# Rotation tables gathered and result rows scattered by GpSimd's indirect transfers

## The reference

```python
x = x + L0_gnn(layernorm(x), adj)      # tanh filter, two 128x128 products, adj product
x = x + L0_ffn(layernorm(x))           # 8 experts 128 -> 256 -> 128, top 2 of 8 by a gate
x = x + L1_gnn(layernorm(x), adj)      # normalised (adj + I) @ x @ w, elu
x = x + L1_ffn(layernorm(x))           # causal attention, then 8 experts 128 -> 341 -> 128, top 2
# in the attention, for 4 query heads and 2 key heads of 32 dimensions:
q = q * cos + rotate_half(q) * sin
k = k * cos + rotate_half(k) * sin
```

## Time and profile before

| | |
|---|---|
| runs | 735.93, 737.3, 740.03 us; median 737.3 us |
| the profiled execution | 740.08 us, its span from the first to the last instruction 738.0 us |
| TensorE busy | 662.6 us (90%) |
| VectorE busy | 551.4 us (75%) |
| ScalarE busy | 319.7 us (43%) |
| GpSimd busy | 135.3 us (18%) |

### The profile page before, as it was taken

One profiled execution on the slowest core, in us unless ns is written; L12 is line 12 of the kernel. 1 busy time (PEld: TensorE's weight loads), 2 busy tenths in 40 slices (PEclk: granted clock), 3 DMA queues, 4 the chain that ended last, 5 costly groups with the idle time before them and its releaser, 6 DMA issues. The chain is left out here.

```text
span 738.0 us, 13217 instructions
## 1 busy us (share of the span) xinstructions
PE 662.6 (90%) x4749; PEld 339.5 (46%) x4749; DVE 551.4 (75%) x1231; ACT 319.7 (43%) x472; POOL 135.3 (18%) x178
## 2 busy tenths in 40 slices
PE   3999889999958998787899999979778999999997
PEld 2433324777744454332322322423244666666665
DVE  7898485899993366778666766682679888888886
ACT  0554305799930111021322433546445556555554
POOL 2000040243630222002060000010012142324200
PEclk9999989999997999969899999999899899999999
DMA  8950000001014011001120000000000010000001
GB/s 324 418 237 1 9 21 15 16 16 29 15 28 98 0 32 33 1 0 33 27 64 29 1 1 0 2 0 2 0 1 9 22 31 30 1 28 28 0 0 57
DMA packets 18173, 30.65 MB, mean 42 GB/s; under 512 B 5024, under 2 KB 14800, under 8 KB 15824
## 3 DMA queue, kind: packets, MB, share of 16 engines
q1 hardware_dynamic: 16672, 29.84, 12.0%
q10 hardware_dynamic: 1456, 0.22, 0.2%
HBM read 26.63 MB, written 1.05 MB: 38 GB/s over the span
## 5 line engine op out<-in xcount | busy, mean ns | idle before, releaser
L1252 PE MATMUL ps<-xT,A 128*128 128x512 f16 (+1 forms) x576 | 133.1, 386 | 7.1 <-DVEq L1764 4.3
L1648 DVE TENSOR_REDUCE A<-ps 128x1 f32<-128x512 f32 (+3 forms) x160 | 92.5, 608 | 42.3 <-PE ps L1125 41.7
L801 ACT ACTIVATE A<-ps 128x1024 f32<-128x1024 f32 (+3 forms) x80 | 68.7, 895 | 81.6 <-PE ps L1192 81.6
L1252 PEld LDWEIGHTS ps<-xT,A 128*128 128x128 f16 (+1 forms) x576 | 59.9, 107 | 67.5 <-DVEq L1764 4.8
L1774 DVE SCALAR_TENSOR_TENSOR A<-ps,A 128x512 f32<-128x512 f32 (+1 forms) x96 | 65.6, 683 | 31.8 <-ACT A L831 26.5
L831 ACT ACTIVATE A<-ps 128x512 f32<-128x512 f32 (+1 forms) x96 | 57.1, 595 | 54.6 <-PE ps L1252 54.5
L1267 PE MATMUL ps<-A 128*128 128x128 f16 (+1 forms) x1152 | 71.8, 222 | 4.1 <-DVE R L1730 2.3
L839 ACT ACTIVATE A<-A 128x512 f16<-128x512 f32 (+1 forms) x96 | 59.8, 623 | 33.6 <-DVE A L1774 33.6
L1267 PEld LDWEIGHTS ps<-A 128*128 128x128 f16 (+1 forms) x1152 | 68.6, 99 | 11.7 <-issue 2.6
L1781 DVE TENSOR_TENSOR A<-A 128x512 f16<-128x512 f32 (+1 forms) x96 | 72.0, 750 | 0.1
L566 POOL TENSOR_TENSOR A<-A,factor 128x682 f32<-128x682 f32 (+3 forms) x32 | 38.5, 1216 | 146.7 <-PE ps L1267 90.4
(11 more groups left out here) (202 smaller groups left out, 814.4 us busy)
## 6 DMA issues: line engine op xcount, KB each, us to landing
A<-in_adj_t SPq DMA_DIRECT2D x16, 1024.0 KB, 22.9
A<-in_f_w SPq DMA_DIRECT2D x16, 170.5 KB
A<-A SPq DMA_DIRECT2D x72, 32.0 KB, 1.8
R<-in_f_w SPq DMA_DIRECT2D x16, 128.0 KB, 2.1
x<-in_x_in SPq DMA_DIRECT2D x4, 256.0 KB, 4.6
R<-in_cos_t SPq DMA_DIRECT2D x4, 256.0 KB, 4.5
R<-in_sin_t SPq DMA_DIRECT2D x4, 256.0 KB, 7.9
A<-in_f_w SPq DMA_DIRECT2D x8, 128.0 KB
```

Of the source, the lines that this page charges most:

```text
L801: act.activation(Pb[:, n % 2, 2 * pair:2 * pair + 2, t0:CW], ps[:, 2 * pair:2 * pair + 2, t0:CW], ACT.Exp, scale=1.0 / (SQ * SQ * float(HD ...
L1252: last = pe.matmul(ps[0:r, 3 * m + k, :], w[:, s, m, k0:k0 + r], a[:, CW * g:CW * g + CW], start=(n == 0), stop=(n == 2))
L1648: dve.reduce_max(pm[:, h, t % TPC, b:b + 1], ps[:, bank, 0:width], AX_X).then_inc(s_rmf, 1)
```

## The change

The eight table copies by SyncE become two indirect gathers by GpSimd: for each of the 128 partitions p it reads row p mod 32 of the table. The row numbers are made by an iota on GpSimd and an AND on VectorE (`head_dim`). GpSimd waits for `s_add0` ahead of them, as SyncE did, and they raise a new semaphore, `s_tab`, for which VectorE waits beside `s_attw`. The four stores by SyncE become sixteen indirect scatters by GpSimd, one for each tile of 128 rows of 512 bytes, with the row numbers in `row_at`.

```diff
@@ -116,6 +116,8 @@
+        row_at = sb("row_at", [P, NT], I32)
+        head_dim = sb("head_dim", [P, 1], I32)
@@ -496,9 +500,6 @@
             sp.wait_ge(s_add0, E0 * NC + 2)
-            for dst, src in ((cos_sb, cos_t), (sin_sb, sin_t)):
-                for h in range(NH):
-                    sp.dma_start(dst[HD * h:HD * h + HD, :], src).then_inc(s_attw, 16)
             for dst, src in ((wq32, wq), (wk32, wk), (wv32, wv), (wo32, wo), (wr32, w_router)):
                 sp.dma_start(dst, src).then_inc(s_attw, 16)
@@ -526,10 +527,6 @@
-            for g in range(NC):
-                sp.wait_ge(s_add1, (E1 - 1) * NC + g + 1 + 2)
-                sp.dma_start(out[:, TPC * g:TPC * g + TPC, :], x[:, TPC * g:TPC * g + TPC, :]).then_inc(s_out, 16)
-            sp.wait_ge(s_out, 16 * NC)
@@ -545,6 +542,10 @@
+            pool.iota(row_at[:, :], pattern=[[1, NT]], base=0, channel_multiplier=NT).then_inc(s_const, 1)
+            pool.iota(head_dim[:, :], pattern=[[0, 1]], base=0, channel_multiplier=1).then_inc(s_const, 1)
+            pool.wait_ge(s_const, 4)
@@ -609,6 +610,13 @@
+            pool.wait_ge(s_add0, E0 * NC + 2)
+            pool.wait_ge(s_hd, 1)
+            for dst, src in ((cos_sb, cos_t), (sin_sb, sin_t)):
+                pool.indirect_dma_start(out=dst, out_offset=None, in_=src,
+                                        in_offset=bass.IndirectOffsetOnAxis(ap=head_dim[:, 0:1], axis=0),
+                                        bounds_check=HD - 1).then_inc(s_tab, 16)
@@ -653,6 +661,13 @@
             chain.loop_ends(E1 // 2 - 1, 6)
+            rows_out = out.rearrange("p t d -> (p t) d")
+            for g in range(NC):
+                pool.wait_ge(s_add1, (E1 - 1) * NC + g + 1 + 2)
+                for t in range(TPC * g, TPC * g + TPC):
+                    pool.indirect_dma_start(out=rows_out, out_offset=bass.IndirectOffsetOnAxis(ap=row_at[:, t:t + 1], axis=0),
+                                            in_=x[:, t, :], in_offset=None, bounds_check=T - 1).then_inc(s_out, 16)
+            pool.wait_ge(s_out, 16 * NT)
@@ -1409,6 +1424,8 @@
+            dve.wait_ge(s_const, 4)
+            dve.tensor_scalar(head_dim[:, :], head_dim[:, :], HD - 1, None, ALU.bitwise_and).then_inc(s_hd, 1)
@@ -1514,7 +1531,8 @@
-            dve.wait_ge(s_attw, 16 * (2 * NH + 5))
+            dve.wait_ge(s_tab, 32)
+            dve.wait_ge(s_attw, 16 * 5)
```

More of the change, by code:

```diff
@@ L238, in program @@
         s_cpool = sem("pool_steps")
+        s_hd = sem("head_dimension_ready")
+        s_tab = sem("rotation_tables_loaded")
         s_dve = sem("vector_steps")
```

## The result

The changed kernel takes 749.7 us (median of four runs, 749.1 to 757.8), the kernel before 737.6 us beside it: a ratio of 1.0183 with a 95% interval of 1.0141 to 1.0226. The loss is 12.1 us; 6.3 us were forecast. A ratio is taken over the undisturbed runs and a median over all of them, so the one need not be the quotient of the others. The profiled execution after has a span of 748.1 us, 738.0 before.

The account below looks back on a forecast made before the run. TensorE, busy 90% of the span, was taken as the bound, its last expert block's matmuls ending the chain. Stores +6.2 us, with the AND +6.3, tables 0: 737.3 + 6.3 = 743.6 us, range 739.8 to 757.0.

Parts of the forecast that it names:

- the small additions: Two iotas on GpSimd at the start, costing nothing, and one AND on VectorE at 105 us, 0.1 us on the path.
- The tables: Two gathers on GpSimd from 221.4 us, hidden in idle time, 0 us; VectorE may go on as late as 240.1.
- The rival with late tables: Second gather lands after 240.1 and TensorE waits in the second graph stage; 2 us at 8 us per gather; chance 0.05.
- The stores: Sixteen GpSimd scatters at the kernel's end, 4.4 us per chunk with a backlog, last issue at 741.64: +6.2 us.
- N: Time one scatter holds GpSimd, put at 1.1 us; between 1.06 and 1.38 the stores cost 12N - 7.0 us.
- The last L1797 "still at about 735": Sign in the profile after: VectorE's last add still at about 735 us; well after would mean port or tables.
- The rival with the shared port: VectorE and GpSimd hold each other up in the tail: +8.0 us if VectorE loses, +10.0 if GpSimd waits; chance 0.15.
- scatters of differing length while VectorE works: Sign in the tail that the forecast is wrong and the port is at work; sixteen transfers of equal length were forecast.
- the other form of the port rival: In the tail GpSimd waits for VectorE, 0.7 us for each scatter issued before 735: end at 748.0, +10.0 us.
- the cheap case: Rival at the stores: a scatter holds GpSimd no longer than SyncE's store issue, 0.34 us: +1.0 us; chance 0.17.
- the case that was thought most likely: The forecast itself, at the stores: one scatter takes 0.8 to 1.5 us, +3.7 to +11.5 us; chance 0.45.
- a slow issue: Rival at the stores: one scatter takes 2 to 3.35 us, all 16 in one line: +19.5 to +41 us; chance 0.18.

Follow-up runs that it names:

- the four wide scatters: Changed kernel with tables copied by SyncE and the stores as four GpSimd scatters of 2 KB rows instead of sixteen of 512 B: 740.5 us beside 737.9 (ratio 1.0043).
- the late case: Changed kernel with tables copied by SyncE and all 16 scatters waiting for the last chunk: +24.1 us on the kernel before (ratio 1.0298).

## Why the prediction was right or wrong, point by point

- **What bounds it, and the small additions: right.** The iotas took 0.14 and 0.12 us in the idle time at the start, the AND 0.14 us with the next instruction 0.06 us behind it. The kernel with gathers only bounds both and the tables together at about nothing (ratio 1.002, tail 15.0 us).
- **The tables: right, with the sizes near.** The gathers held GpSimd from 220.45 to 223.16 (221.4 to 223.6 forecast), and the tables had landed 7.4 us after G was written, as the last weight had before. L1530 beside them took 4.24 us for 16 against 4.20: the 1.3 us kept for the shared port were not needed. The weights landed after 1.7 to 1.9 us instead of 7.0 to 8.2, and were not waited for, as said. The rival with late tables falls.
- **The stores: right mechanism, mis-sized term.** The single line of scatters on GpSimd, the backlog over the chunks and the end behind the last landing are as forecast. N was put at 1.1 us; the execution is 0.98 us, but GpSimd idles 0.30 us between two, so that the step is 1.29 us. The sum priced one instruction by its length and had no pause; the nearest rows, the powers with means of 1.0 to 1.3 us, say nothing of a pause between two transfers. With 1.29 us it makes 8.5 us by the formula of the prediction. It also started a scatter at the moment its add ended: 0.87 us lie between, a term put at nothing. These, and 0.35 us more for the first scatter, put chunk 0's scatters past the add of chunk 1, so all sixteen stand in one line; with 0.25 us more for the fifth they make 9.3 us instead of 6.2.
- **From the last issue to the end: mis-sized.** Taken over from SyncE's stores as 2.6 us (2.1 us to the landing and 0.5 us behind it); it is 3.4 us. The bytes don't come later: by the DMA view the last are moved at 745.7, 1.0 us behind the last issue, and before the change at 736.7, 1.3 us behind it. What grows is the time after them, and not with scatters alone: with plain transfers of GpSimd, which landed 1.9 us after their start, it is 3.2 us too, and with the four wide scatters 735.5 - 732.43 = 3.1 us, of which about 2.3 go to the landing (3.3 from the start). The extra time comes with GpSimd as the issuer, not with "indirect"; its cause is open, as the trace gives no landing for the sixteen.
- **The last L1797 "still at about 735": wrong.** It ends at 735.44, but this execution was 2.7 us ahead; counted from chunk 0 it comes 3.1 us late. The rival with the shared port had such a delay (3.9 us), but its mechanism fails: GpSimd's computing beside the same steps delays nothing, VectorE's L1799 beside the scatters take 0.67 to 0.73 us against 0.68, and plain transfers from GpSimd, four at a time, delay nothing. What delays the add is a wait of engines for TensorE beside a row of eight indirect transfers, which none of the rivals had. It costs 2.7 us.
- **The sign "scatters of differing length while VectorE works": there, but small.** Behind VectorE's last add a scatter takes 0.98 us, and 1.26 where it is the first of a line. Beside its work they take up to 1.33 us in the changed kernel and up to 1.93 us with scatters only. So GpSimd may well wait for VectorE, as the other form of the port rival has it, but for 0.3 us in all in the changed kernel and 1.5 us with scatters only, counted against the same scatters of the late case; the rival had put 0.7 us on each. That the port does it no run shows.
- **The two rules cited.** The pace of a scatter speaks against the one that would have made the cheap case: the Trainium skill, DMA: Bandwidth & Descriptors, section "Anatomy of one DMA — SWDGE (gpsimd) path", calls the making of the descriptors "small, variable", and here a scatter of 128 rows holds GpSimd for 0.98 us and comes every 1.29 us, the larger part of the loss. The trace doesn't tell how much of it is the making of descriptors. The other, that VectorE with two SBUF inputs contends with GpSimd's reads (the Trainium skill, SBUF — State Buffer, section "Who interferes with whom"), would fit the longer scatters beside VectorE, and no run isolates it.
- **The sum, and luck.** 6.3 us forecast; measured are 9.3 for the line, 2.7 for the stall and 0.8 behind the last issue. The 749.7 us lie inside the range of 739.8 to 757.0, but the loss is above the case that was thought most likely (+3.7 to +11.5 us) and near twice the sum. The upper part of the range was kept for a slow issue and for the port; neither came at its price, and what filled it was the longer step, the 0.87 us ahead of the first scatter and a stall that none of the rivals had. So that it held is in part luck.

## What to carry to other kernels

In these runs an indirect transfer of 128 rows costs GpSimd 1.29 us in a line, 0.98 us of work and 0.30 us of pause. Rows of 2 KB took the same 0.98 us as rows of 512 B, and the second gather with rows of 8 KB took 1.01 us, so put as many bytes in a row as the layout gives (2 KB rows cut the loss from 12.8 to 1.9 us), and use an indirect transfer only where the rows are not known beforehand. At the end of a program count each issue of the queue that stores the result: with an issue step longer than the chunks' spacing divided by their transfers, the chunks queue up and the whole line is added. A row of eight indirect transfers also held up engines that compute beside it, so look at the waits of the others, not at GpSimd's alone.

## What was not expected of the hardware

- GpSimd idles 0.30 us between two indirect transfers and none between two plain ones (four in 2.13 us).
- With eight indirect transfers back to back, scatters or gathers, an engine that waits for TensorE is idle for 3.8 to 5.7 us that end on nothing the trace names, in six of six traces that have such a row beside TensorE's work; with four, in a row or spread out, or with sixteen plain transfers in fours, in none. Its cause is open.
- The gathers of 1 MB into 128 partitions moved faster than the copies into 32: the last one landed 9.4 us after the first issue (220.45 to 229.86), against 11.6 us from 218.42 to the landing of the last sine copy before (issued at 221.6, landed 8.4 us later).
